# Spreading 1/std of the large layer norms: two rounded products of 512 columns and diagonal parts from VectorE, in place of four full products of 128

## The chip, the cores and the metric

One core of one Trainium2 chip. The metric is the time of one execution in device microseconds (us). Names of engines: PE is TensorE (PEld its weight loads), DVE is VectorE, ACT is ScalarE, POOL is GpSimd, SP is SyncE.

## The reference

Input x is 32 batches x 32 tokens x 256 channels, cond is 32 x 256. In short:

```python
x = x + conv(x, cond)                       # each batch causal, 32 lags, one weight per channel and lag
ada = cond @ ada_w + ada_b                  # shift1, scale1, gate1, shift2, scale2, gate2
x1 = ln(x) * (1 + scale1) + shift1          # ln(x) = (x - mean) * rsqrt(var + 1e-6) over 256 channels
q, k, v = split(x1 @ qkv_w + qkv_b)         # 16 heads of 128
x = x + gate1 * (attention(q, k, v) @ out_w + out_b)
x2 = ln(x) * (1 + scale2) + shift2
x = x + gate2 * (gelu(x2 @ ffn_w1 + b1) @ ffn_w2 + b2)
# and the block's result is added to its input once more
```

## The kernel before

Activations lie transposed: 128 channels on the partitions, tokens in the columns, two channel tiles (`ct` 0 and 1). The 1024 tokens are worked on in two halves of 512. A layer norm therefore sums over partitions, and does it with matrix products.

Large products are done in three rounded products each (`three`, L943 to L947; `v_tile` L949 to L956): weights and activations are split into a high part rounded to fp32r and a low part (`wh`, `wl`, `x1h`, `x1l`, `oh`, `ol`, `hh`, `hl`), and high x low, low x high and high x high are added in PSUM. ACT makes the high parts, POOL the low parts of the weights (L294) and of half of the hidden tiles (L332), DVE the low parts of the activations.

There are five norms. Norms 0 and 1 take 256 tokens each and the change leaves them alone. Norms 2, 3 and 4 take 512 tokens each ("large"): norm 2 is the first norm of the second half of the tokens, norms 3 and 4 are the second norm of the first and the second half. A large norm goes through these steps:

- `mean(n)` (L886): four rounded products of `ones_r` (every element 1/256) with high and low input parts, L894, put the mean into all partitions of a PSUM bank. `centre(n)` (L574, DVE) subtracts it, `squares(n)` (ACT, L388) squares.
- `var(n)` (L904): small products on PE, then on DVE `var_eps(n)` (L588): a transpose (L594) into `vt` and an addition (L597), so that `ve` holds var + eps of 512 tokens as 128 partitions x 4.
- `rstd(n)` (L301, POOL): power of -0.5 by L304, into `rs`, 128 x 4.
- `spread(n)` (L918, PE): for each of 4 columns k one full fp32 product of 128 columns, L925, with `rs[:, k]` broadcast as weights and the unit matrix `ident` moving. It puts 1/std of 512 tokens into all partitions of the bank.
- DVE: `norm(n)` multiplies (L604), `shift(n)` adds (L611), and after ACT's `x1_high(n)` (L398) `x1_low(n)` subtracts (L623). `scale_up(n)` (L585) has been done earlier.

Every engine has its own program, written out by hand in its order, and they meet at counting semaphores. PE's order around a spread: norms 2 and 3 are worked in between products of other work in rounds U = 3 and U = 5 of the loop at L1077 (`attend`, `var`, `out_proj(U-1, 0)`, `attend(U-1, 3)`, `out_proj(U-1, 1)`, `spread`, `out_proj(U-1, 2)`). Norm 4 lies in the second product of the feed-forward part for the first half (L1172 to L1180):

```python
for k in range(MT):            # MT = 8
    ffn2(0, k)
    ffn2(1, k)                 # 6 products of 512 columns for each k
    if k == 1: var(4)
    if k == 3: spread(4)
ffn1(1, range(MT))             # waits for x1_low(4), both channel tiles
```

On DVE the order is `var_eps`, `o_low` twice (L671), `norm` for norms 2 and 3, and `hidden_low(0, 7)`, `var_eps(4)`, `norm(4)` for norm 4. On POOL `rstd(2)` and `rstd(3)` stand ahead of the low parts of the next round's query weights, `rstd(4)` ahead of `hidden_low(1, 0)`. SP only starts loads and stores.

Of the kernel before, what the change touches and what calls it, by code (L numbers as in the profile page):

```python
# [5 lines left out]
F32 = mybir.dt.float32  # L6
F32R = mybir.dt.float32r
ALU = mybir.AluOpType
# [3 lines left out]
P = 128  # L12
# [4 lines left out]
def cond_resid_block_kernel(nc, x, cond, ada_w, ada_b, qkv_w, qkv_b, out_w, out_b,  # L17
# [5 lines left out]
    B, T, C = x.shape  # L23
# [8 lines left out]
    TG = HT // P  # L32
# [24 lines left out]
    NORMS = CHUNKS + [(0, HT), (HT, HT)]  # L57
# [13 lines left out]
    with ExitStack() as ctx:  # L71
        def sb(name, shape, dt=F32):
            return ctx.enter_context(nc.sbuf_tensor(name, shape, dt))

        def sem(name):
            return ctx.enter_context(nc.semaphore(name))
# [3 lines left out]
        x1h = sb("x1h", [P, CT, TOK], F32R)  # L80
        x1l = sb("x1l", [P, CT, TOK], F32R)
# [11 lines left out]
        ident = sb("ident", [P, P])  # L93
        ones = sb("ones", [P, P])
        ones_r = sb("ones_r", [P, P], F32R)
# [8 lines left out]
        rc = sb("rc", [P, GH * TG])  # L104
        ve = sb("ve", [P, TG])
        rs = sb("rs", [P, TG])
        mhalf = sb("mhalf", [P, TG])
        vt = sb("vt", [P, TG, T])

# [32 lines left out]
        s_in, s_mean, s_xm, s_sq = sem("ln_input"), sem("ln_mean"), sem("ln_centred"), sem("ln_squares")  # L142
        s_var, s_ve, s_rs, s_rb = sem("ln_var"), sem("ln_var_eps"), sem("ln_rstd"), sem("ln_rstd_spread")
        s_vt = sem("ln_var_transposed")
        s_sc, s_mod, s_x1f = sem("ln_scaled"), sem("ln_normed"), sem("x1_full")
        s_hi, s_lo = sem("x1_high"), sem("x1_low")
        s_whi = [sem(f"{n}_weights_high") for n in ("q", "k", "v", "o")]
# [13 lines left out]
        def part(t, ct, span):  # L161
            return t[:, ct, span[0]:span[0] + span[1]]
# [14 lines left out]
        def ln_c(n, ct):  # L177
            return part(yacc if n < NC else x0, ct, NORMS[n])
# [6 lines left out]
        STAT_BANK = [S_BANK, S_BANK, S_BANK, S_BANK, OB[0]]  # L185
# [89 lines left out]
        @block.gpsimd  # L275
        def _(g):
            g.memset(ident[:, :], 0.0).then_inc(s_id0, 1)
            g.wait_ge(s_id0, 1)
            g.affine_select(out=ident[:, :], in_=ident[:, :], compare_op=ALU.not_equal, fill=1.0,
                            base=0, pattern=[[-1, P]], channel_multiplier=1).then_inc(s_const, 1)  # L280
            g.memset(ones[:, :], 1.0 / C).then_inc(s_const, 1)
            g.memset(mhalf[:, :], -0.5).then_inc(s_const, 1)
            g.wait_ge(s_const, 3)

            g.wait_ge(s_cond, 1)
            for d, ct in BY_POOL:
                j = DIAG_LAGS[d]
                g.tensor_scalar(diag[:, CT * d + ct, :], ident[:, :], condT[:, ct, T - 1 - j:T - j], 0.0,
                                ALU.mult, ALU.add).then_inc(s_diag[1], 1)

            def low_part(U, p):
                i, cols = p // 2, slice(PIECE * p, PIECE * (p + 1))
                g.wait_ge(s_whi[i], 2 * U + p % 2 + 1)
                g.tensor_tensor(wl[:, cols], raw[:, cols], wh[:, cols].bitcast(F32), ALU.subtract)\  # L294
                    .then_inc(s_wlo[i], 1)

            def low_parts(U, i):
                low_part(U, 2 * i)
                low_part(U, 2 * i + 1)

            def rstd(n):  # L301
                nt = NORMS[n][1] // P
                g.wait_ge(s_ve, n + 1)
                g.tensor_tensor(rs[:, 0:nt], ve[:, 0:nt], mhalf[:, 0:nt], ALU.pow).then_inc(s_rs, 1)  # L304


            g.wait_ge(s_in, CT)
            low_parts(0, 0)
            low_part(0, 2)
            rstd(0)  # L310
            low_part(0, 3)
            g.wait_ge(s_lo, CT)
            low_part(0, 4)
            rstd(1)
            low_part(0, 5)
            low_parts(0, 3)
            g.memset(pt[:, :, :, :], 0.0).then_inc(s_zero, 1)
            for i in range(3):
                low_parts(1, i)
            for U in range(1, NU):  # L320
                if U == 3:
                    rstd(2)
                if U == 5:
                    rstd(3)
                low_parts(U + 1, 0)
                low_parts(U + 1, 1)
                low_parts(U, 3)
                low_parts(U + 1, 2)

            def hidden_low(n, m):  # L330
                g.wait_ge(s_hhi, MT * n + m + 1)
                g.tensor_tensor(hl[:, m, :], hf[:, m % 4, :], hh[:, m, :].bitcast(F32), ALU.subtract)\  # L332
                    .then_inc(s_hlo[0], 1)

            for m in (0, 2):
                hidden_low(0, m)
            low_parts(NU, 3)
            for m in (4, 6):
                hidden_low(0, m)
            rstd(4)  # L340
            for m in (0, 2, 4, 6):
                hidden_low(1, m)
# [187 lines left out]
        def _(v):  # L530
# [57 lines left out]
            def var_eps(n):  # L588
                v.wait_ge(s_var, n + 1)
                if n < 2:  # L590
                    nt = NORMS[n][1] // P
                    v.tensor_scalar(ve[:, 0:nt], STAT_BANK[n][:, 0:nt], EPS, None, ALU.add).then_inc(s_ve, 1)
                else:
                    v.transpose(vt[:, :, :], STAT_BANK[n][:, 0:P].rearrange("p (k r) -> p k r", r=T))\  # L594
                        .then_inc(s_vt, 1)
                    v.wait_ge(s_vt, n - 1)
                    v.tensor_scalar(ve[:, :], vt[:, :, 0:1].rearrange("p k r -> p (k r)"), EPS, None, ALU.add)\  # L597
                        .then_inc(s_ve, 1)

            def norm(n):  # L600
                v.wait_ge(s_rb, n + 1)
                v.wait_ge(s_sc, CT * (n + 1))
                for ct in range(CT):
                    v.tensor_tensor(ln_c(n, ct), ln_c(n, ct), STAT_BANK[n][:, 0:NORMS[n][1]], ALU.mult)\  # L604
                        .then_inc(s_mod, 1)

            def shift(n):
                for ct in range(CT):
                    v.wait_ge(s_mod, CT * n + ct + 1)
                    c = by_batch(ln_c(n, ct))  # L610
                    v.tensor_tensor(c, c, ada(SHIFT1 if n < NC else SHIFT2, ct, NORMS[n]), ALU.add)\  # L611
                        .then_inc(s_x1f, 1)
# [55 lines left out]
            def o_low(U, h):  # L668
                v.wait_ge(s_ohi, GH * U + h + 1)
                row = B_V + GH * (U % NG) + h  # L670
                v.scalar_tensor_tensor(out=ol[:, h, :], in0=OB[h % 2][:, :], scalar=bT[:, row:row + 1],  # L671
                                       in1=oh[:, h, :].bitcast(F32), op0=ALU.add, op1=ALU.subtract)\
                    .then_inc(s_olo, 1)
# [84 lines left out]
            scale_up(2)  # L758
            var_eps(2)
            o_low(2, 2)  # L760
            o_low(2, 3)
            norm(2)
            shift(2)
            x1_low(2)
# [15 lines left out]
            scale_up(3)  # L780
            var_eps(3)
            o_low(4, 2)
            o_low(4, 3)
            norm(3)
            shift(3)
# [19 lines left out]
            def hidden_low(n, m):  # L805
                v.wait_ge(s_hhi, MT * n + m + 1)
                v.tensor_tensor(hl[:, m, :], hf[:, m % 4, :], hh[:, m, :].bitcast(F32), ALU.subtract)\
                    .then_inc(s_hlo[1], 1)
# [11 lines left out]
            scale_up(4)  # L820
            hidden_low(0, 7)
            var_eps(4)
            norm(4)
            shift(4)
            x1_low(4)
# [30 lines left out]
        def _(pe):  # L856
            pe.wait_ge(s_const, 1)
            pe.wait_ge(s_row[0], 16)
            for ct in range(CT):
                m = pe.transpose(S_BANK[:, B * ct:B * (ct + 1)], crow[:, ct * P:(ct + 1) * P], ident[0:B, 0:B])  # L860
            m.then_inc(s_condt, 1)
            for n in range(2):
                t0, nt = CHUNKS[n][0] // P, CHUNKS[n][1] // P
                pe.wait_ge(s_x[n], 16)
                for ct in range(CT):
                    for t in range(nt):
                        m = pe.transpose((OB, YB)[n][ct][:, t * P:(t + 1) * P], xtok[:, t0 + t, ct * P:(ct + 1) * P], ident[:, :])  # L867
# [48 lines left out]
                m.then_inc(s_var, 1)  # L916

            def spread(n):  # L918
                pe.wait_ge(s_rs, n + 1)
                for k in range(NORMS[n][1] // P):  # L920
                    if n < 2:
                        dst = STAT_BANK[n][:, k * P:(k + 1) * P]
                    else:
                        dst = STAT_BANK[n][:, :].rearrange("p (t k r) -> p k t r", t=TG, r=T)[:, k]
                    m = pe.matmul(dst, rs[:, k:k + 1].to_broadcast([P, P]), ident[:, :], start=True, stop=True)  # L925
                m.then_inc(s_rb, 1)

# [114 lines left out]
            for ct in range(CT):  # L1042
                for t in range(TG):
                    m = pe.transpose(OB[ct][:, t * P:(t + 1) * P], xtok[:, TG + t, ct * P:(ct + 1) * P], ident[:, :])
# [127 lines left out]
            for k in range(MT):  # L1172
                if k == MT // 2:
                    pe.wait_ge(s_wlo[3], 2 * NU + 2)
                ffn2(0, k)
                ffn2(1, k)
                if k == 1:
                    var(4)
                if k == 3:
                    spread(4)  # L1180
            ffn1(1, range(MT))
            pe.wait_ge(s_fin, CT)
# [49 lines left out]
```

## Time and profile before

| what | value |
|---|---|
| median of 3 runs | 312.3 us (312.1 to 313.58) |
| the profiled execution | 311.81 us |
| its span, first to last instruction | 310.0 us |
| PE busy | 298.0 us (96%) |
| PEld busy | 251.9 us |
| DVE busy | 180.2 us |
| ACT busy | 174.5 us |
| POOL busy | 120.4 us |
| granted TensorE clock | 1.000 |

Busy times overlap; an engine's time counts only where the others wait for it. The duration of a matrix product in a row is longer than the distance from its start to the next start, because products are pipelined: distances of starts are what PE's time is made of. A full fp32 product shows as two rows each of PE and PEld.

### The profile page before, as it was taken

To read this page: it belongs to the slowest core of one execution; us is meant where nothing else is said; L and a number is where in the kernel's file an instruction comes from. 1 tells how busy PE (TensorE), PEld (TensorE's weight loads), DVE (VectorE), ACT (ScalarE), POOL (GpSimd) and SP (SyncE) were. 2 spreads that over 40 slices of the span, in tenths; PEclk is the share of its full clock that TensorE was granted. 3 is DMA by queue.
4 is the path that set the end of the run, shared out by engine and by line. 5 is a ranking of instruction groups with operands and counts; after the bars stand their busy time and mean duration, and the time that the engine had idled before them with its cause. 6 is when DMAs were issued, how large, how long until landed. Compare 5 with 4: busy or idle time off the path is not lost.

```text
span 310.0 us, 6149 instructions
## 1 busy us (share of the span) xinstructions
PE 298.0 (96%) x2604; PEld 251.9 (81%) x2604; DVE 180.2 (58%) x303; ACT 174.5 (56%) x316; POOL 120.4 (39%) x103
## 2 busy tenths in 40 slices
PE   4978999999999999999999999999999999899995
PEld 3875997878898888788888888888898888678885
DVE  3997698987866745472546554341620556957232
ACT  5752568434762855486376736644762794625901
POOL 5007729331911544072337305531821671611400
PEclk9999999999999999999999999999999999999999
DMA  7903321400160061007004300610150020000012
GB/s 231 362 27 79 112 84 57 150 0 2 43 231 0 2 229 45 0 4 271 1 2 153 120 2 2 213 59 2 59 212 2 2 68 3 0 0 3 0 68 68
DMA packets 15259, 23.00 MB, mean 74 GB/s; under 512 B 792, under 2 KB 8320, under 8 KB 15232
## 3 DMA queue, kind: packets, MB, share of 16 engines
q1 hardware_dynamic: 15184, 22.58, 21.6%
q8 instruction: 20, 0.33, 0.4%
q10 hardware_dynamic: 48, 0.03, 0.1%
q14 instruction: 7, 0.06, 0.1%
HBM read 21.57 MB, written 1.05 MB: 73 GB/s over the span
## 4 chain that ended last, share of the span: by engine, by line
PE 85%; DVE 9%; POOL 3%; ACT 1%; DMA 1%; issue 1%; DVEq 0%; POOLq 0%
PE bank L945 18%; PE bank L947 18%; PE bank L946 18%; PE bank L1019 9%; DVE xc L548 6%; PE bank L953 5%; PE bank L954 4%; PE bank L955 4%; PE bank L1003 3%; POOL wl L294 3%; PE bank L925 1%; DVE x1l L617 1%; PE bank L894 1%; DMA crow<-in_cond_dram 1%; PE bank L867 1%
## 5 line engine op out<-in xcount | busy, mean ns | idle before, releaser
L294 POOL TENSOR_TENSOR wl<-raw,wh 128x512 fp32r<-128x512 f32 x72 | 98.7, 1398 | 133.2 <-ACT wh L357 116.5
L408 ACT ACTIVATE pool<-bank,bT 128x512 f32<-128x512 f32 x56 | 38.5, 688 | 54.3 <-PE bank L947 54.3
L945 PE MATMUL bank<-x1h,wl 128*128 128x512 f32 (+1 forms) x176 | 66.3, 377 | 0.8 <-DVE x1l L623 0.4
L947 PE MATMUL bank<-x1h,wh 128*128 128x512 f32 (+1 forms) x176 | 65.1, 370 | 0.0
L946 PE MATMUL bank<-x1l,wh 128*128 128x512 f32 (+1 forms) x176 | 65.1, 370 | 0.0
L671 DVE SCALAR_TENSOR_TENSOR ol<-bank,bT,oh 128x512 fp32r<-128x512 f32 x32 | 24.0, 750 | 36.6 <-ACT oh L433 35.6
L357 ACT ACTIVATE wh<-raw 128x512 fp32r<-128x512 f32 x72 | 40.9, 621 | 3.5 <-PE bank L947 3.5
L548 DVE SCALAR_TENSOR_TENSOR xc<-x,condT,xc 128x496 f32<-128x496 f32 (+27 forms) x82 | 42.8, 592 | 0.1
L945 PEld LDWEIGHTS bank<-x1h,wl 128*128 128x128 f32 x176 | 33.2, 188 | 7.1 <-DVE x1l L623 0.8
L947 PEld LDWEIGHTS bank<-x1h,wh 128*128 128x128 f32 x176 | 33.2, 188 | 5.7
L946 PEld LDWEIGHTS bank<-x1l,wh 128*128 128x128 f32 x176 | 33.2, 189 | 5.4
L1019 PEld LDWEIGHTS bank<-pt,pool 128*128 128x128 f32 x256 | 32.1, 191 | 2.0 <-issue 0.3
L1019 PE MATMUL bank<-pt,pool 128*128 128x128 f32 x256 | 32.5, 275 | 0.0
L433 ACT ACTIVATE oh<-bank,bT 128x512 fp32r<-128x512 f32 x32 | 22.0, 686 | 10.0 <-PE bank L1019 10.0
L945 PE MATMUL bank<-oh,wl 128*128 128x512 f32 x64 | 26.8, 418 | 0.2 <-DVE ol L671 0.2
L953 PE MATMUL bank<-wh,x1l 128*128 128x512 f32 x64 | 25.9, 404 | 0.0
L947 PE MATMUL bank<-oh,wh 128*128 128x512 f32 x64 | 25.1, 392 | 0.0
L946 PE MATMUL bank<-ol,wh 128*128 128x512 f32 x64 | 25.0, 390 | 0.0
L954 PE MATMUL bank<-wl,x1h 128*128 128x512 f32 x64 | 24.9, 389 | 0.0
L955 PE MATMUL bank<-wh,x1h 128*128 128x512 f32 x64 | 24.9, 389 | 0.0
L643 DVE TENSOR_REDUCE mx<-bank 128x16 f32<-128x512 f32 x8 | 5.5, 692 | 32.4 <-PE bank L1003 32.4
L666 DVE STREAM_TRANSPOSE pt<-pnorm 32x512 f32<-32x512 f32 (+1 forms) x36 | 23.2, 644 | 1.2
(121 smaller groups left out, 421.5 us busy)
## 6 DMA issues: line engine op xcount, KB each, us to landing
raw<-in_L_cond_qkv_w_dram SPq DMA_DIRECT2D x24, 512.0 KB, 5.6
raw<-in_L_cond_out_w_dram SPq DMA_DIRECT2D x8, 512.0 KB, 3.7
raw<-in_L_cond_ffn_w_dram SPq DMA_DIRECT2D x4, 512.0 KB, 5.1
adaw<-in_L_cond_ada_w_dram SPq DMA_DIRECT2D x1, 1024.0 KB, 10.8
out_dram<-pool SPq DMA_DIRECT2D x3, 256.0 KB, 2.2
pool<-in_x_dram SPq DMA_DIRECT2D x2, 256.0 KB, 3.1
adaw<-in_L_cond_ada_w_dram SPq DMA_DIRECT2D x1, 512.0 KB, 5.4
pool<-in_x_dram SPq DMA_DIRECT2D x1, 512.0 KB, 6.2
```

Of the source, the lines that this page charges most:

```text
L294: g.tensor_tensor(wl[:, cols], raw[:, cols], wh[:, cols].bitcast(F32), ALU.subtract)\
L357: a.activation(wh[:, cols], raw[:, cols], ACT.Copy).then_inc(s_whi[i], 1)
L408: a.activation((q_sb if j < GH else k_sb)[:, j % GH, :], src, ACT.Identity, bias=bias(U, j // GH, j % GH)).then_inc(s_ev, 1)
L548: m = v.scalar_tensor_tensor(out=acc[:, :, j:], in0=xs[:, :, :T - j], scalar=w, in1=(acc if i else xs)[:, :, j:], op0=ALU.mult, op1=ALU.add)
L671: v.scalar_tensor_tensor(out=ol[:, h, :], in0=OB[h % 2][:, :], scalar=bT[:, row:row + 1], in1=oh[:, h, :].bitcast(F32), op0=ALU.add, op1=A ...
L945: pe.matmul(dst, wl[:, w_cols], a_hi, start=start, stop=False)
L946: pe.matmul(dst, wh[:, w_cols], a_lo, start=False, stop=False)
L947: return pe.matmul(dst, wh[:, w_cols], a_hi, start=False, stop=stop)
L953: pe.matmul(dst, x1l[:, kt, tk], wh[:, wc], start=(kt == 0), stop=False)
L954: pe.matmul(dst, x1h[:, kt, tk], wl[:, wc], start=False, stop=False)
L955: m = pe.matmul(dst, x1h[:, kt, tk], wh[:, wc], start=False, stop=(kt == CT - 1))
L1019: m = pe.matmul(OB[h % 2][:, t * P:(t + 1) * P], v_sb[:, t, h * P:(h + 1) * P], pt[:, h, t, :], start=True, stop=True)
```

## The change

For norms 2 to 4 `spread(n)` becomes two rounded products of 512 columns: `ones_r` as weights and, moving, a matrix that carries 1/std times 256 on a diagonal for each of the 4 columns, once its high part (in `x1h`) and once its low part (in `x1l`), added in PSUM. DVE makes these in a new `rstd_diagonal(n)`: `rsh` = 256 rs rounded, `rsl` the rest, and `ident` times each of them, spread over 512 columns. For norms 2 and 3 `rstd_diagonal` stands between the two last `o_low`, for norm 4 behind `var_eps(4)`. POOL waits behind `rstd(n)` until both diagonal parts are written. In the feed-forward part `spread(4)` moves from behind k == 3 to behind k == 4. Norms 0 and 1 are as before.

```diff
@@ gpsimd
                 g.tensor_tensor(rs[:, 0:nt], ve[:, 0:nt], mhalf[:, 0:nt], ALU.pow).then_inc(s_rs, 1)
+                if n >= 2:
+                    g.wait_ge(s_rd, 2 * (n - 1))
@@ vector
+            def rstd_diagonal(n):
+                v.wait_ge(s_rs, n + 1)
+                v.tensor_scalar(rsh[:, :], rs[:, :], float(C), None, ALU.mult).then_inc(s_rh, 1)
+                v.wait_ge(s_rh, n - 1)
+                v.scalar_tensor_tensor(out=rsl[:, :], in0=rs[:, :], scalar=float(C), in1=rsh[:, :].bitcast(F32),
+                                       op0=ALU.mult, op1=ALU.subtract).then_inc(s_rl, 1)
+                eye = ident[:, :].rearrange("p (t r) -> p t r", r=T).unsqueeze(2).to_broadcast([P, TG, TG, T])
+                for t, r in ((x1h, rsh), (x1l, rsl)):
+                    if r is rsl:
+                        v.wait_ge(s_rl, n - 1)
+                    dst = part(t, 0, NORMS[n]).rearrange("p (t k r) -> p t k r", t=TG, r=T)
+                    by_k = r[:, :].bitcast(F32).unsqueeze(1).unsqueeze(3).to_broadcast([P, TG, TG, T])
+                    v.tensor_tensor(dst, eye, by_k, ALU.mult).then_inc(s_rd, 1)
...
             o_low(2, 2)
+            rstd_diagonal(2)
             o_low(2, 3)
...
             o_low(4, 2)
+            rstd_diagonal(3)
             o_low(4, 3)
...
             var_eps(4)
+            rstd_diagonal(4)
             norm(4)
@@ tensor
             def spread(n):
+                if n >= 2:
+                    for i, t in enumerate((x1h, x1l)):
+                        pe.wait_ge(s_rd, 2 * (n - 2) + i + 1)
+                        m = pe.matmul(STAT_BANK[n][:, :], ones_r[:, :], part(t, 0, NORMS[n]),
+                                      start=(i == 0), stop=(i == 1))
+                    m.then_inc(s_rb, 1)
+                    return
                 pe.wait_ge(s_rs, n + 1)
...
-                if k == 3:
+                if k == 4:
                     spread(4)
```

The order of the instructions at norm 2 on DVE (`ol` is the low part of the attention output, `yacc` the working copy in the norm), first before, then with the change:

```order
L597 TENSOR_SCALAR ve<-vt 128x4 [waits ln_var_transposed]
L671 SCALAR_TENSOR_TENSOR ol<-bank,bT,oh 128x512 [waits attn_out_high] x2
L604 TENSOR_TENSOR yacc<-yacc,bank 128x512 [waits ln_scaled,ln_rstd_spread]
L604 TENSOR_TENSOR yacc<-yacc,bank 128x512
L611 TENSOR_TENSOR yacc<-yacc,adaT 128x512 [waits ln_normed] x2
```

```order
L603 TENSOR_SCALAR ve<-vt 128x4 [waits ln_var_transposed]
L693 SCALAR_TENSOR_TENSOR ol<-bank,bT,oh 128x512 [waits attn_out_high]
L610 TENSOR_SCALAR rsh<-rs 128x4 [waits ln_rstd]
L612 SCALAR_TENSOR_TENSOR rsl<-rs,rsh 128x4 [waits ln_rstd_high]
L620 TENSOR_TENSOR x1h<-ident,rsh 128x512
L620 TENSOR_TENSOR x1l<-ident,rsl 128x512 [waits ln_rstd_low]
L693 SCALAR_TENSOR_TENSOR ol<-bank,bT,oh 128x512 [waits attn_out_high]
L626 TENSOR_TENSOR yacc<-yacc,bank 128x512 [waits ln_scaled,ln_rstd_spread]
L626 TENSOR_TENSOR yacc<-yacc,bank 128x512
```

Four DVE instructions came in ahead of the last `ol`.

The order on PE at norm 4 (`hh`, `hl` are the hidden activations), before and with the change:

```order
L945 MATMUL bank<-hh,wl 128x512 [waits hidden_low_odd]
L946 MATMUL bank<-hl,wh 128x512
L947 MATMUL bank<-hh,wh 128x512
L925 MATMUL bank<-ident,rs 128x4x32 [waits ln_rstd]
L925 MATMUL bank<-ident,rs 128x4x32 x3
L945 MATMUL bank<-hh,wl 128x512 [waits hidden_low_even,o_weights_low]
```

```order
L974 MATMUL bank<-hh,wl 128x512 [waits hidden_low_even,o_weights_low]
L975 MATMUL bank<-hl,wh 128x512
L976 MATMUL bank<-hh,wh 128x512
L974 MATMUL bank<-hh,wl 128x512 [waits hidden_low_even]
L975 MATMUL bank<-hl,wh 128x512
L976 MATMUL bank<-hh,wh 128x512
L947 MATMUL bank<-x1h,ones_r 128x512 [waits ln_rstd_on_diagonal]
L947 MATMUL bank<-x1l,ones_r 128x512 [waits ln_rstd_on_diagonal]
```

The spread moved behind six products of `ffn2` that stood behind it.

On POOL the instruction behind the power of norm 2, the same at norm 3, with the change:

```order
L307 TENSOR_TENSOR rs<-ve,mhalf 128x4 [waits ln_var_eps]
L297 TENSOR_TENSOR wl<-raw,wh 128x512 [waits q_weights_high,ln_rstd_on_diagonal]
L297 TENSOR_TENSOR wl<-raw,wh 128x512 [waits q_weights_high]
```

The first low part of the weights now waits for the diagonal parts too.

## Rows read from the trace of the kernel before

**Rows 1.** The page: busy time of PE, and the chain by engine.

```profile
PE 298.0 (96%) x2604; PEld 251.9 (81%) x2604; DVE 180.2 (58%) x303; ACT 174.5 (56%) x316; POOL 120.4 (39%) x103
...
PE 85%; DVE 9%; POOL 3%; ACT 1%; DMA 1%; issue 1%; DVEq 0%; POOLq 0%
```

**Rows 2.** Busy time by stretch: us, then each engine's busy us, clock, DMA.

```profile
112.00:130.00 18.00, 18.00 (x113) 15.40 (x112) 9.67 (x16) 9.07 (x15) 3.58 (x4) 1.00 0.28 99
170.00:190.00 20.00, 20.00 (x244) 16.96 (x243) 9.46 (x17) 11.00 (x18) 4.50 (x4) 1.00 0.15 56
```

**Rows 3.** Timeline of PE at norm 2's spread: start, us, instruction.

```profile
122.03 0.40 PE L947 MATMUL bank<-oh,wh 128*128 128x512 f32 x1
122.27 1.05 PE L925 MATMUL bank<-ident,rs 128*128 128x128 f32 x8
...
123.39 0.39 PE L946 MATMUL bank<-ol,wh 128*128 128x512 f32 x1
```

**Rows 4.** Timeline of PE at norm 2's mean.

```profile
111.74 0.39 PE L894 MATMUL bank<-x1h,ones_r 128*128 128x512 f32 x1
111.96 0.61 PE L894 MATMUL bank<-x1l,ones_r 128*128 128x512 f32 x2
112.42 0.39 PE L945 MATMUL bank<-x1h,wl 128*128 128x512 f32 x1
```

**Rows 5.** Timeline of DVE and POOL at norm 2.

```profile
118.63 0.32 DVE L594 STREAM_TRANSPOSE vt<-bank 128x128 f32<-128x128 f32 x1 [0.20 <-PE bank L914]
118.98 0.17 DVE L597 TENSOR_SCALAR ve<-vt 128x4 f32<-128x4 f32 x1
119.06 0.75 DVE L671 SCALAR_TENSOR_TENSOR ol<-bank,bT,oh 128x512 fp32r<-128x512 f32 x1
121.80 0.75 DVE L671 SCALAR_TENSOR_TENSOR ol<-bank,bT,oh 128x512 fp32r<-128x512 f32 x1 [1.99 <-ACT oh L433]
...
119.23 1.01 POOL L304 TENSOR_TENSOR rs<-ve,mhalf 128x4 f32<-128x4 f32 x1 [7.16 <-DVE ve L597]
120.21 2.53 POOL L294 TENSOR_TENSOR wl<-raw,wh 128x512 fp32r<-128x512 f32 x2
132.76 2.55 POOL L294 TENSOR_TENSOR wl<-raw,wh 128x512 fp32r<-128x512 f32 x2 [10.02 <-ACT wh L357]
```

**Rows 6.** Timeline of PE, POOL and DVE at norm 3.

```profile
178.52 1.05 PE L925 MATMUL bank<-ident,rs 128*128 128x128 f32 x8
...
175.49 1.01 POOL L304 TENSOR_TENSOR rs<-ve,mhalf 128x4 f32<-128x4 f32 x1 [7.16 <-DVE ve L597]
```

**Rows 7.** Timeline of PE at norm 4, and the first product that needs its result.

```profile
275.44 1.05 PE L925 MATMUL bank<-ident,rs 128*128 128x128 f32 x8
...
276.56 0.40 PE L946 MATMUL bank<-hl,wh 128*128 128x512 f32 x1
...
281.84 0.40 PE L945 MATMUL bank<-x1h,wl 128*128 128x512 f32 x1
```

**Rows 8.** Timeline of DVE and POOL at norm 4.

```profile
276.53 1.29 DVE L604 TENSOR_TENSOR x<-x,bank 128x512 f32<-128x512 f32 x2 [2.57 <-PE bank L925]
...
279.12 1.30 DVE L623 TENSOR_TENSOR x1l<-x,x1h 128x512 fp32r<-128x512 f32 x2
...
274.04 1.01 POOL L304 TENSOR_TENSOR rs<-ve,mhalf 128x4 f32<-128x4 f32 x1 [4.88 <-DVE ve L597]
```

**Rows 9.** Timeline where PE did wait for a low part: DVE, then PE.

```profile
30.43 0.76 DVE L623 TENSOR_TENSOR x1l<-yacc,x1h 128x256 fp32r<-128x256 f32 x2
...
31.25 0.38 PE L945 MATMUL bank<-x1h,wl 128*128 128x256 f32 x1 [0.45 <-DVE x1l L623]
31.47 0.28 PE L946 MATMUL bank<-x1l,wh 128*128 128x256 f32 x1
```

**Rows 10.** Timeline of DVE and POOL ahead of norm 4's mean.

```profile
264.83 3.18 DVE L617 TENSOR_TENSOR x1l<-yacc,x1h 128x512 fp32r<-128x512 f32 x2 [0.21 <-ACT x1h L393]
262.33 3.44 POOL L294 TENSOR_TENSOR wl<-raw,wh 128x512 fp32r<-128x512 f32 x2 [6.67 <-ACT wh L357]
```

More of the change, by code:

```diff
@@ L106, in cond_resid_block_kernel @@
         rs = sb("rs", [P, TG])
+        rsh = sb("rsh", [P, TG], F32R)
+        rsl = sb("rsl", [P, TG], F32R)
         mhalf = sb("mhalf", [P, TG])
@@ L144, in cond_resid_block_kernel @@
         s_vt = sem("ln_var_transposed")
+        s_rh, s_rl, s_rd = sem("ln_rstd_high"), sem("ln_rstd_low"), sem("ln_rstd_on_diagonal")
         s_sc, s_mod, s_x1f = sem("ln_scaled"), sem("ln_normed"), sem("x1_full")
@@ L918, in spread @@
             def spread(n):
+                if n >= 2:
[5 more added lines that the diff above has]
+                    return
                 pe.wait_ge(s_rs, n + 1)
                 for k in range(NORMS[n][1] // P):
[L921 to L924, printed above, removed]
+                    dst = STAT_BANK[n][:, k * P:(k + 1) * P]
                     m = pe.matmul(dst, rs[:, k:k + 1].to_broadcast([P, P]), ident[:, :], start=True, stop=True)
```

## The prediction

> **What bounds the kernel now.** I read the page first: PE is busy for 298.0 of 310.0 us, and 85% of the chain that ended last is PE's [rows 1]. What matters is whether it is so at the three places of the change, so the table of stretches comes next: around norms 2 and 3 PE is busy for 18.00 of 18.00 and 20.00 of 20.00 us, at the full clock [rows 2]. In these stretches a microsecond taken from PE's queue is a microsecond of the kernel, unless PE then waits for somebody. Last I read the timelines at each norm, PE first, then DVE and POOL, and looked for the slack that the new instructions may use up.
>
> **What PE loses.** Norm 2 shows the price of the old spread by starts: from the start of the last product ahead of it (122.03) to the start of the second product behind it (123.39) pass 1.36 us, and in it lie that product, the spread, and one product behind it [rows 3]. A rounded product of 512 columns takes one start to the next in 0.23 us: the last three of the mean's four take 0.68 with the first, (112.42 - 111.74) / 3 = 0.227, three starts being visible [rows 4]; those with `ones_r` as weights are exactly the new kind. Four intervals (the product ahead, two of the new spread, one behind) are 0.92, so a spread saves 1.36 - 0.92 = 0.44 us. The old spread at norm 3 has the same 1.05 row [rows 6], and norm 4 shows 275.44 to 276.56, 1.12 for spread and one product, against 3 x 0.23 = 0.69: 0.43 [rows 7]. **Three spreads: minus 1.31 us**, all of it on PE's queue.
>
> **What DVE gains, norms 2 and 3.** POOL's power ends at 119.23 + 1.01 = 120.24 [rows 5]. From DVE to POOL a result takes 0.08 (118.98 + 0.17 = 119.15 to 119.23); I take the same back: DVE starts at 120.32. `rsh` is an instruction on 128 x 4 like `ve`, 0.17, to 120.49; a dependent one starts 0.03 later (118.95 to 118.98), an independent one 0.08 behind the start before it (118.98 to 119.06) [rows 5]. So `rsl` starts at 120.52 and the first product with `ident` at 120.60. These two have no row. The nearest is a DVE product or subtraction on 128 x 512, 0.69 for one and 1.29 for two in a row, so 0.60 from start to start [rows 8]. The far end is such an instruction next to a busy POOL, 3.18 for two, 1.59 each [rows 10]. I take 0.69 and 0.60, since POOL is made to wait and is idle then. The parts are written at 121.29 and 121.89. PE wants them at 122.27 and 122.50, and loads the weights of a product about one interval, 0.23, ahead; even the second weight load, at 122.27, is 0.33 after PE can know (121.89 + 0.05, the way of 31.19 to 31.25 in [rows 9]). The last `o_low` can start at 121.80, just behind, as before [rows 5]: it waited there for ACT for 1.99 us, and this wait is the cover of all four new instructions. Gone, each norm would cost about what DVE runs over. Norm 3 has the same distances, its power at 175.49 and its spread at 178.52 (3.03, against 3.04 at norm 2) [rows 6]. **Zero at both.**
>
> **What POOL's wait costs.** Behind it stand two low parts of query weights, now at 120.21 [rows 5]; they go back to 121.95, 1.7 us later, and end near 124.5. The next POOL work comes at 132.76, after 10.02 us of idle time [rows 5], and these weights are for the next round. DVE's shift instructions at norm 2 will start near 124.2 and may meet the last of it; by the rate of [rows 10] that is 0.9 us at most on a result which the next round needs. SP's next load of these weights stands behind another wait in the same queue. **Zero.**
>
> **Norm 4** has least room. POOL's power ends at 275.05 [rows 8]; by the same steps the parts are written at 276.10 and 276.70. PE's place for the spread is now six products later: 275.44 + 6 x 0.23 = 276.81. The first product is in time; the second's weight load is due at 276.81, and PE can know at 276.75. It fits with 0.06 to spare. Without the move to k == 4 PE would have waited 1.3 us here. The second product starts at 277.04, its row lasts 0.39 [rows 4], so DVE's norm starts at about 277.47 in place of 276.53 [rows 8]: 0.94 later. The last low part then ends at 279.12 + 1.30 + 0.94 = 281.36 in place of 280.42. The product that waits for it was due at 281.84 [rows 7], and now is at 281.84 - 0.44 = 281.40, with its weight load at 281.17. PE knows at 281.42. A product that had to wait this way started its stream late: at norm 0 the next start came 0.22 behind, where 0.12 is usual [rows 9], so 0.10. It starts at 281.52 instead of 281.40: **plus 0.12 us**. So the move takes 1.42 us of slack almost exactly. DVE's next steps (sums and gating for the first half) are 0.9 later too, but PE needs them only behind eight more tiles.
>
> **The sum:** -1.31 + 0.12 = -1.2 us. Against the profiled execution, 311.81, that is 310.6; its own time lies 0.5 below the median of the runs, 312.3, and against that median it is **311.1 us**, 0.4% less.
>
> **A rule weighed against a row.** Two DVE instructions in a row overlap by 0.09 us (1.29 for two of 0.69) [rows 8]. The Trainium skill, VectorE: DVE Perf Modes, section "The DRAIN you can't avoid", says that the next operation does not start before the pipe has emptied (and that an operation not held may start earlier). By that the second diagonal part of norm 4 would be there 0.09 later, PE would wait by about 0.13 for it, and the sum would be -1.1; by the row it is -1.2. I keep the row.
>
> **Rivals.**
>
> A. *The diagonal parts are late and PE waits at all three spreads* (slower). Each part reads `ident` in a pattern that repeats and one value per 32 columns, a form without a row here; if it costs d, then at norms 2 and 3 the second is written 2d after 120.60, PE waits from d = 0.84 on, and at norm 4 from 0.67 on. Six parts: the waits come to 6d - 4.7, and pass the 1.2 saved at about d = 1.0. At the far end of 1.59 [rows 10] they are 4.8, less 1.2, so about 315.9. For it: nothing but the missing row; against it: DVE's instructions of 512 columns all take about 0.69 while POOL rests, and broadcast operands (`adaT`, L611) stand among them. From 1.0 us on it decides; chance 0.07.
>
> B. *The gain is half eaten at norm 4*: PE waits 0.3 to 1.0 us for the second part or for the last low part, because slack there is 0.06 at one place and -0.25 at the other. Any 0.1 to 0.3 us that I missed on the chain POOL, DVE, PE, DVE, ACT, DVE counts in full: 311.4 to 312.1. For it: the rows leave no room; against: only one place of three. Chance 0.16.
>
> C. *A collision falls otherwise*: ahead of norm 4's mean DVE takes 3.18 us for two subtractions beside a POOL that works from 262.33 to 265.77, and PE stands [rows 10]. They start within fractions of a microsecond of each other, and one of the two at 0.69 would bring PE forward by 0.9: -2.1, so 310.2. The Trainium skill, SBUF — State Buffer, section "Who interferes with whom", has it that the order of issue decides which of the two engines blocks; this row shows a block of 0.9 for each, and none that fell the other way. For it: the phase may change; against: everything there is started by PE, so the shift of 0.88 keeps the distances. Chance 0.10.
>
> **How the numbers follow.** The forecast (310.8 to 311.4) has 0.67; a median may lie 0.3 off on top of that. The unknown costs: if the far end of a part (1.59) holds, that is rival A; the near end is in the sum, and nothing excludes 0.1 of extra gain. A measurement of this kernel can tell about 0.5%, 1.6 us, from no change. Faster by that: rival C, and a few of the forecast's cases with luck in the median, 0.13. Slower: A, 0.06 with a rest. All else is within 0.5%, 0.81. The range of 8 in 10 takes in C and most of B and the scatter of medians of some 0.3: 310.1 to 312.3.
>
> **What would show it.** The two new product rows 0.23 apart, no PE wait for a diagonal part, at norm 2 the last `o_low` still at its distance of 3.1 us from the transpose of the variance; two DVE rows of 0.69 for `x1h` and `x1l` from `ident`; PE's weight load for the first feed-forward product of the second half waiting for DVE's low part by 0.1 to 0.3 us; span 308.8. Wrong would be: DVE rows above 0.85 (A), a PE wait above 0.5 at norm 4 (B), a different length of the two DVE subtractions ahead of norm 4's mean (C).

## The result, and the profile of the changed kernel

| | before | changed |
|---|---|---|
| median | 312.31 us (16 runs, 311.72 to 313.58) | **314.36 us** (16 runs, 311.72 to 316.59) |
| ratio | 1 | **1.0049** [1.0031, 1.0067] |
| profiled execution, its span, granted clock | 311.81, 310.0, 1.000 | 315.42, 313.6, 0.989 |

Slower by 0.5%, where 311.1 us (310.1 to 312.3) was forecast. The page of the changed kernel, its busy times, the queue that brings in instructions and the chain by engine (to be held against [rows 1]):

```profile
PE 300.4 (96%) x2586; PEld 253.4 (81%) x2586; DVE 185.7 (59%) x315; ACT 174.6 (56%) x316; POOL 121.0 (39%) x103
...
q8 instruction: 20, 0.33, 0.5%
...
PE 85%; DVE 8%; POOL 3%; issue 1%; ACT 1%; DMA 1%; DVEq 0%; POOLq 0%
```

PE issues 18 products and 18 weight loads fewer and is nevertheless busy for 2.4 us more. The three places of the change do not explain that. Norm 3 (to be held against [rows 6]), PE, then DVE, then POOL (start, duration, instruction, idle time before it and its releaser):

```profile
178.66 0.40 PE L976 MATMUL bank<-oh,wh 128*128 128x512 f32 x1
178.90 0.39 PE L947 MATMUL bank<-x1h,ones_r 128*128 128x512 f32 x1
179.13 0.39 PE L947 MATMUL bank<-x1l,ones_r 128*128 128x512 f32 x1
179.35 0.39 PE L974 MATMUL bank<-oh,wl 128*128 128x512 f32 x1
...
176.90 0.17 DVE L610 TENSOR_SCALAR rsh<-rs 128x4 fp32r<-128x4 f32 x1 [0.47 <-POOL rs L307]
177.11 0.16 DVE L612 SCALAR_TENSOR_TENSOR rsl<-rs,rsh 128x4 fp32r<-128x4 f32 x1
177.19 0.68 DVE L620 TENSOR_TENSOR x1h<-ident,rsh 128x512 fp32r<-128x512 f32 x1
177.79 0.68 DVE L620 TENSOR_TENSOR x1l<-ident,rsl 128x512 fp32r<-128x512 f32 x1
...
178.55 2.55 POOL L297 TENSOR_TENSOR wl<-raw,wh 128x512 fp32r<-128x512 f32 x2 [1.68 <-DVE x1l L620]
```

The two products start 0.23 apart and wait for nobody, the diagonal parts take 0.68 each, 0.60 from start to start, and POOL stands back for 1.68 us: all as forecast. Norm 4 (against [rows 7, 8]), DVE and PE, and the first product that needs its result:

```profile
279.69 0.69 DVE L620 TENSOR_TENSOR x1l<-ident,rsl 128x512 fp32r<-128x512 f32 x1
...
280.62 0.40 PE L947 MATMUL bank<-x1h,ones_r 128*128 128x512 f32 x1
280.85 0.39 PE L947 MATMUL bank<-x1l,ones_r 128*128 128x512 f32 x1
...
285.05 0.40 PE L976 MATMUL bank<-hh,wh 128*128 128x512 f32 x1
285.28 0.43 PE L974 MATMUL bank<-x1h,wl 128*128 128x512 f32 x1
285.56 0.39 PE L975 MATMUL bank<-x1l,wh 128*128 128x512 f32 x1
```

No wait at the spread; at the first feed-forward product of the second half the next start comes 0.28 later in place of 0.23, so 0.05 is lost.

To find the 3.6 us by which the span is longer I laid the two PE timelines side by side and took the start of the same product in both:

| place | before | changed | difference |
|---|---|---|---|
| a product at 34 us, long before the change's first place | 33.59 | 34.46 | +0.87 |
| second product behind the spread of norm 2 | 123.39 | 123.81 | +0.42 |
| second product behind the spread of norm 3 | 179.64 | 179.58 | -0.06 |
| last product ahead of the scores of round U = 5 | 187.39 | 187.29 | -0.10 |
| first product behind these scores | 188.93 | 190.97 | **+2.04** |
| 13 products later | 192.00 | 195.63 | **+3.63** |
| ahead of norm 4's spread | 274.52 | 278.30 | +3.78 |
| behind it | 277.72 | 281.08 | +3.36 |
| last tiles | 297.79 | 301.30 | +3.51 |

The spreads bring -0.45, -0.48 and -0.42, together -1.35 (the second product behind is taken, because before the first one after a full spread still takes 0.31 to the next start in place of 0.23). The loss arises in the attention scores of round 5, 128 small products in 1.2 us that the change does not touch, and right behind them. PE there, before and changed:

```profile
187.71 1.30 PE L1003 MATMUL bank<-pool 128*32 128x32 f32 x128
188.93 0.51 PE L953 MATMUL bank<-wh,x1l 128*128 128x512 f32 x1
```

```profile
187.60 1.26 PE L1032 MATMUL bank<-pool 128*32 128x32 f32 x125
190.78 0.25 PE L1032 MATMUL bank<-pool 128*32 128x32 f32 x3 [1.92 <-issue]
190.97 0.50 PE L982 MATMUL bank<-wh,x1l 128*128 128x512 f32 x1
...
192.23 0.62 PE L984 MATMUL bank<-wh,x1h 128*128 128x512 f32 x1
192.64 0.63 PE L982 MATMUL bank<-wh,x1l 128*128 128x512 f32 x1
```

After 125 of the 128 products PE stands for 1.92 us, and the releaser is "issue": no engine and no transfer of data that the profile knows of. A little later products of 0.39 take 0.63 and start 0.43 apart in place of 0.23. The table of stretches of the changed kernel (us, PE busy, PEld, DVE, ACT, POOL, granted clock, DMA share, GB/s) shows both causes:

```profile
188.00:188.50 0.50, 0.50 (x80) 0.50 (x72) 0.00 (x0) 0.50 (x2) 0.00 (x0) 1.00 0.16 33
188.50:189.00 0.50, 0.37 (x45) 0.26 (x31) 0.00 (x0) 0.50 (x2) 0.09 (x1) 1.00 0.00 0
189.00:189.50 0.50, 0.00 (x0) 0.00 (x0) 0.00 (x0) 0.34 (x1) 0.50 (x1) 1.00 0.00 0
...
192.00:192.50 0.50, 0.50 (x3) 0.46 (x2) 0.49 (x1) 0.00 (x0) 0.00 (x0) 0.73 0.00 0
192.50:193.00 0.50, 0.50 (x2) 0.38 (x2) 0.00 (x0) 0.48 (x1) 0.00 (x0) 0.50 0.00 0
195.50:196.00 0.50, 0.50 (x3) 0.36 (x3) 0.47 (x2) 0.50 (x1) 0.50 (x2) 0.86 0.00 0
```


First, just behind the start of the scores a transfer begins; then PE stands, from 188.86 to 190.78. Second, from about 192.2 to 195.6, behind this standstill, the granted clock is 0.50, the lower of the two levels (1.2 of 2.4 GHz), which costs the 1.6 us between +2.04 and +3.63. The remaining +0.87 at 34 us is an early delay with a clock of 0.84 from 25 to 30 us; the same kernel's second profile below is without it (33.59, as before), and b_diag below, whose PE does the work of before, is 2.47 behind at 33 us with a clock of 1.00, so I count early delays as scatter.

Which transfer? The view of the DMA queues from 187 to 191 us shows one packet of the queue of instructions (16 KB; 20 such packets carry PE's program: 0.33 MB) in the slice from 188.1 on (each GB/s number is a fortieth of the stretch; the last row is the queue's packets, MB and share), and none from 178 to 187 us:

```profile
GB/s 0 0 0 0 0 0 0 0 0 0 0 164 0 0 0 0 0 0 0 0 0 0 0 0 0 0 0 0 0 0 0 0 0 0 0 0 0 0 0 0
...
q8 instruction: 1, 0.02, 2.1%
```

Before, the view from 178 to 183 us has the corresponding packet at 179.9, 7.8 us ahead of the same scores, and none from 186 to 190:

```profile
GB/s 0 0 0 0 0 0 0 0 0 0 0 0 0 0 0 131 0 0 0 0 0 0 0 0 0 0 0 0 0 0 0 0 0 0 0 0 0 0 0 0
...
q8 instruction: 1, 0.02, 1.1%
```

This gave **theory S** (stream): PE's program comes in blocks of 16 KB. Each product is two instructions (a PE and a PEld row), a full fp32 product four; each large spread so went from 16 instructions to 4. Norms 2 and 3 put the code of the scores of round 5 24 instructions earlier in the stream. These scores run 256 instructions in 1.2 us, and now the fetch of the block in which they end starts only with them (0.6 us behind their first product, where it was 7.8 us ahead of it before). The Trainium skill, Runtime: NRT & Kernel Launch, section "Instruction fetch mechanics", describes such blocks of 256 instructions and calls the cost of crossing a boundary "mostly hidden"; here it is not.

### The profile page after: what moved, and what is told of

Its sections match the earlier page's. It is cut to its first block, busy times and chain, and to the rows that moved or that the text cites. A ratio compares the mean times of both kernels' runs of the same rounds, so it can differ in the third digit from the quotient of the medians.

```text
span 313.6 us, 6128 instructions
## 1 busy us (share of the span) xinstructions
PE 300.4 (96%) x2586; PEld 253.4 (81%) x2586; DVE 185.7 (59%) x315; ACT 174.6 (56%) x316; POOL 121.0 (39%) x103
## 4 chain that ended last, share of the span: by engine, by line
PE 85%; DVE 8%; POOL 3%; issue 1%; ACT 1%; DMA 1%; DVEq 0%; POOLq 0%
PE bank L974 18%; PE bank L976 18%; PE bank L975 18%; PE bank L1048 9%; DVE xc L554 6%; PE bank L982 5%; PE bank L984 5%; PE bank L983 4%; PE bank L1032 3%; POOL wl L297 3%; DVE x1l L639 1%; PE bank L919 1%; DMA crow<-in_cond_dram 1%; PE bank L892 1%; PE bank L939 1%
## 5 line engine op out<-in xcount | busy, mean ns | idle before, releaser
L984 PE MATMUL bank<-wh,x1h 128*128 128x512 f32 x64 | 25.6, 400 | 0.0
```

What stands on the lines that cost most here:

```text
L984: m = pe.matmul(dst, x1h[:, kt, tk], wh[:, wc], start=False, stop=(kt == CT - 1))
```

## The experiments

All were timed against before on the chip they ran on. Twelve kernels in three jobs; before had 311.86 us in the first job, 312.66 in the second, 312.86 in the third (29, 35 and 35 runs), its fastest 311.68, 311.94 and 311.92. Many executions, of before too, carry early delays of 1 to 2.5 us, ahead of every place of the change, so beside medians I give the fastest runs where they lie close together. `s_fill` is a semaphore that nobody waits for; adding to it does no work and takes one place in PE's instruction stream.

**1. a_same**, the changed kernel again.

> The changed kernel once more, as the control. Theory S (the code stream of PE): the 24 machine instructions that PE no longer has before the attention scores of round U = 5 move these scores against the 16 KB blocks in which PE's code is fetched, so that one fetch starts only inside the scores and PE stands about 1.9 us there, and TensorE's clock falls to half for 3.4 us behind it. It then expects the stall at the scores of U = 5 in this profile too, and a time 1 to 3 us above before. Rival R (chance of a run: DMA, start of the early norms): no stall at that place in this profile, or one at another place, and the same in before's.

Measured: 313.83 us median, ratio 1.0051 [1.0024, 1.0079], so the loss repeats on another chip. PE's timeline:

```profile
186.88 1.26 PE L1032 MATMUL bank<-pool 128*32 128x32 f32 x125
189.69 0.25 PE L1032 MATMUL bank<-pool 128*32 128x32 f32 x3 [1.54 <-issue]
```

PE stands behind the same 125th product. The same products against before: -0.83 at the last product ahead of the scores, +0.94 at the first behind them, so the standstill costs 1.77. The clock stays at 1.00 here; it fell in the profile where the wait was 1.92.

**2. a_fill12**: in `three`, one addition in front of each of the 12 products behind each spread of norms 2 to 4, so that PE's stream is as long as before's ahead of the scores.

```diff
@@ spread(n), n >= 2
+                    fillers[0] += 12
+            def filler():
+                if fillers[0]:
+                    fillers[0] -= 1
+                    pe.sem_inc(s_fill, 1)
@@ three
+                filler()
```

> The changed kernel with 12 additions to an unused semaphore on PE's queue, one by one between the 12 products behind each of the three spreads, so that every later instruction of PE stands at the same number in its queue as before the change. Theory S: no stall at the scores of U = 5, no fall of the clock there, and the saving of PE appears, 311.0 to 311.6 us with before at 312.3, so 0.7 to 1.3 us below before and 2 to 4 below the changed kernel. Rival R, or a theory in which the work of VectorE or the new products slow the kernel: the time stays that of the changed kernel, 313 to 315.

Measured: 314.45 us, ratio 1.0062 [1.0036, 1.0087]. This expectation failed: PE still stands.

```profile
189.15 1.16 PE L1044 MATMUL bank<-pool 128*32 128x32 f32 x113
191.96 0.23 PE L1044 MATMUL bank<-pool 128*32 128x32 f32 x4 [1.65 <-issue]
```

But the place is telling. 24 instructions are more in front of it (two spreads), and PE stands behind the 113th product in place of the 125th: 12 products, 24 instructions, earlier. So the standstill belongs to a fixed place in the instruction stream. The fetch still started with the scores (its packet at 189.5). So the place of the boundary alone does not say when the fetch starts.

**3. b_start232**: the kernel before with 232 additions at the head of PE's queue.

```diff
@@ tensor
+            for _ in range(232):
+                pe.sem_inc(s_fill, 1)
```

> The kernel before, its work untouched, with 232 additions to an unused semaphore at the very start of PE's queue, where PE waits 3.4 us for its first input; with blocks of 256 instructions this puts the scores of U = 5 at the same place in a block as in the changed kernel (24 less), without the change. Theory S: a stall of about 1.9 us at the scores of U = 5 and the clock at half behind it, 314 to 316 us. If the additions take longer than the cover, up to 2 us more at the start, seen there. Theories that lay it to the new work: no stall at these scores.

Measured: 348.63 us (346.89 to 350.64); the additions took far more than I had allowed for, PE's first product starts at 36.65 in place of 3.40 us. The time is useless, the timeline is not. Around round 5 no instruction of the change is in the kernel, and PE does this:

```profile
220.93 1.26 PE L1006 MATMUL bank<-pool 128*32 128x32 f32 x125
223.84 0.25 PE L1006 MATMUL bank<-pool 128*32 128x32 f32 x3 [1.64 <-issue]
```

Against the changed kernel 232 + 24 = 256 instructions more lie ahead of this place: exactly one block. **The standstill was put into before's work by the position of its code**; the additions also start all work 33 us later, but that alone would not choose the same 125th product. Theory S holds for the cause.

**4. a_start24**: the changed kernel with 24 additions at the head of PE's queue, where PE waits for the first load anyway.

> The changed kernel with 24 additions to an unused semaphore at the start of PE's queue: scores of U = 5 stand in their block as before the change, the scores of the earlier rounds 12 or 24 instructions later than before. Theory S: no stall at U = 5 and 310.9 to 311.6 us, unless the shift makes a stall in another round, which the profile would show in its scores. Others: 313 to 315.

Measured: 312.25 us, ratio 1.0008 [0.9986, 1.0031]. The scores run through (188.86, x128), with the fetch at 181.5. The first product starts at 4.62 in place of 3.40, so the additions outran their cover by 1.22 us and ate the gain.

**5. b_diag**: before's PE, with DVE's `rstd_diagonal` and POOL's wait, whose results nobody reads (spread behind k == 3).

> VectorE's and GpSimd's part of the change alone: rstd_diagonal and GpSimd's wait are in, the results of it are not read; PE's queue is that of the kernel before (four full products, behind k == 3). Theory S (PE's code stream and its block boundary in the scores of U = 5): as before, within 0.3 us (the norm of n = 4 starts some 0.2 us later on VectorE, within its slack), no stall in the scores of U = 5. Rival V (VectorE's work, or the stopped GpSimd, costs the time): 313 to 314.5.

Measured: 314.16 us (312.26 up; one run at 373.78), ratio 1.0018 [0.9992, 1.0044]: not to be told from before. Its fastest three, 312.26 to 312.38, are 0.3 above before's fastest; the interval alone would still admit 1.4 us. The profile narrows it: its PE is 2.47 us behind before's at 33 us, ahead of every place of the change, 2.42 behind at the scores of round 7, and 2.68 at the last product. So the DVE and POOL parts cost PE nothing up to norm 4 and at most some 0.25 there, and no standstill occurs.

**6. a_pe**: only PE's part. The two products are released by `rs` and multiply what lies in `x1h` and `x1l`, so 1/std is not spread in this kernel.

> PE's part of the change alone: two rounded products behind k == 4 whose moving data is whatever x1h and x1l hold, released by rs as before the change; no rstd_diagonal, no wait on GpSimd, so 1/std of the norms 2 to 4 is not spread and the output is not the reference's. Theory S: PE's queue counts the same instructions as in the changed kernel, so the stall at the scores of U = 5 is there and the time is that of the changed kernel, 312.4 to 314.5. Rival V: without VectorE's work the saving of 1.2 us appears, 310.7.

Measured: 313.2 us, ratio 0.9998 [0.9972, 1.0024], 11 of 12 runs from 312.74 up and one at 310.92. PE stands after 125 of the 128 products, for 1.82 us from start to start. DVE, POOL and their waits are not needed for the standstill. By the ratio this kernel is neither slower nor faster than before, so the saving of 1.2 us that rival V wanted is not there either; in the profile, which has next to no early delay, its last product comes 1.11 us behind before's, as in a_same (0.97).

**7. a_start8** and **8. a_start14**: as 4, with 8 and 14 additions.

> The changed kernel with 8 additions to an unused semaphore at the start of PE's queue, under the cover of PE's wait for its first input (24 of them outran it by 1.2 us, so up to about 15 are free). The block boundary, at which PE stood behind 250 instructions of the scores of U = 5, comes 8 instructions earlier against the program, behind 242. Theory S: if the boundary ahead of the scores now lies in front of a wait that PE's queue passes early, no stall and 310.6; if not, the stall as in the changed kernel but in front of 14 instead of 6 instructions, 312.4 to 314.5. It shows how far the boundary must move.

> The same with 14 additions, still nearly under the cover: boundary behind 236 instructions of the scores of U = 5. Theory S: no stall, since 24 showed none, and without what 24 cost at the start: 310.5 to 310.8 us, 1.2 less than before; the scores of U = 6 and 7 stay free of a stall too. Rival V: 313 to 314.

Measured: 8: 313.95 us, ratio 1.0016 [0.9985, 1.0048]; one run of 12 at 310.91, the others from 312.82 up, though the profile, at 313.44 us, was without a standstill: it is 2.44 us behind before at 33 us already and only 1.61 behind at the last product. So a run above 312.8 need not be one with a standstill. 14: **311.89 us, ratio 0.9970 [0.9944, 0.9995]**; the first product starts at 3.37, so the additions are hidden, and four runs lie at 310.92 to 311.01.

**9. a14_again**, the same as 8 in its own job.

> The version with 14 semaphore additions at the start of PE's queue once more, with more rounds. Theory S (the changed kernel's whole loss is PE's standstill inside the scores of round 5, which depends on where that code lies in PE's instruction stream): median 0.8 to 1.3 us under before, ratio 0.996 to 0.9975, and no product of the scores waiting over 1 us with nobody named. Rival (the earlier 0.997 was scatter between runs): ratio 0.999 to 1.001.

Measured: **311.79 us, ratio 0.9969 [0.9946, 0.9992]**, five of 12 runs at 310.93 to 311.02 where before's fastest are 311.92 to 312.06. The scores run through:

```profile
188.90 1.30 PE L1035 MATMUL bank<-pool 128*32 128x32 f32 x128
```

So the version with 14 additions beats both kernels, by 0.3% of before and, by the ratios to before, 0.8% of the changed kernel.

**10. a8_again**, 8 additions once more, to see whether one kernel can go both ways.

> The version with 8 additions at the start once more. If the code boundary near the scores of round 5 is marginal there, its single runs fall in two groups, one near 310.9 (no standstill) and one from 312.4 up (standstill of 1.7 to 1.9 us): ratio 1.000 to 1.004. Rival (8 additions are as good as 14 and the earlier runs were scatter): ratio 0.996 to 0.998.

Measured: 314.54 us, ratio 1.0053 [1.0033, 1.0072], none of 12 runs below 313.82. The expectation of two groups failed within this job: all 12 are late. That one kernel can go both ways is shown by the two profiles, 7 without and this one with a standstill:

```profile
186.85 1.23 PE L1035 MATMUL bank<-pool 128*32 128x32 f32 x121
190.01 0.27 PE L1035 MATMUL bank<-pool 128*32 128x32 f32 x7 [1.94 <-issue]
```

8 instructions more in front, 4 products fewer ahead of the standstill: 121 = 125 - 4, the rule of experiment 2 once more. Here again the wait was over 1.9 us, and again the clock fell behind it:

```profile
191.50:192.00 0.50, 0.50 (x2) 0.40 (x2) 0.25 (x1) 0.21 (x1) 0.00 (x0) 0.50 0.00 0
```

**11. a14_k3**: 14 additions, the spread of norm 4 back behind k == 3.

> As a14_again, but the spread of norm 4 back behind k == 3. By the prediction's steps PE then waits at norm 4 until the second diagonal part is written, 1.2 to 1.4 us, and gets back what it no longer waits for the last low part (0.12) with the norm started earlier: span 1.1 to 1.3 us above a14_again, ratio to before 1.000 to 1.001. Rival (PE has other slack there, so the move is worth nothing): within 0.3 us of a14_again.

Measured: 312.32 us, ratio 0.9979 [0.9957, 1.0002]; the fastest 311.88, so 0.95 above the fastest of a14_again (the medians differ by 0.5). PE waits for both diagonal parts:

```profile
274.44 0.40 PE L979 MATMUL bank<-hh,wh 128*128 128x512 f32 x1
275.27 0.49 PE L950 MATMUL bank<-x1h,ones_r 128*128 128x512 f32 x1 [0.43 <-DVE x1h L621]
275.87 0.50 PE L950 MATMUL bank<-x1l,ones_r 128*128 128x512 f32 x1
276.20 0.39 PE L977 MATMUL bank<-hh,wl 128*128 128x512 f32 x1
```

1.76 us from the last product ahead to the first behind, in place of 3 x 0.23: 1.07 lost. The move to k == 4 is worth about 1 us and is what lets norm 4 gain at all; the ratio lies lower than expected (0.9979 where 1.000 to 1.001 was put), the distance of the fastest runs near what was expected (1.1 to 1.3).

**12. a14_free**: 14 additions, without POOL's wait behind the power.

```diff
@@ gpsimd
-                if n >= 2:
-                    g.wait_ge(s_rd, 2 * (n - 1))
```

> As a14_again, but without POOL's wait behind the power. If POOL and DVE hinder each other as ahead of norm 4's mean in before (1.59 per DVE subtraction beside a busy POOL), the two diagonal parts take 1.2 to 1.6 us each in place of 0.68 at norms 2 and 3, the second is there 1.1 to 1.8 us later, and PE waits 0.5 to 1.4 us at each of the two: ratio 1.000 to 1.005. Rival (only luck of phase makes them collide): rows of 0.68 and the time of a14_again.

Measured: 314.63 us, ratio 1.0062 [1.0042, 1.0083]; fastest 314.24, 3.3 above the fastest of a14_again. The wait is worth 3 us, but the rows are not those that I expected. Norm 2, DVE, POOL, PE:

```profile
120.79 1.24 DVE L608 TENSOR_SCALAR rsh<-rs 128x4 fp32r<-128x4 f32 x1 [0.47 <-POOL rs L308]
122.06 1.20 DVE L610 SCALAR_TENSOR_TENSOR rsl<-rs,rsh 128x4 fp32r<-128x4 f32 x1
123.19 0.68 DVE L618 TENSOR_TENSOR x1h<-ident,rsh 128x512 fp32r<-128x512 f32 x1
...
120.73 2.52 POOL L298 TENSOR_TENSOR wl<-raw,wh 128x512 fp32r<-128x512 f32 x2
...
122.55 0.40 PE L976 MATMUL bank<-oh,wh 128*128 128x512 f32 x1
123.92 0.50 PE L947 MATMUL bank<-x1h,ones_r 128*128 128x512 f32 x1 [0.97 <-DVE x1h L618]
124.53 0.50 PE L947 MATMUL bank<-x1l,ones_r 128*128 128x512 f32 x1
```

The two 128 x 512 parts take 0.68; it is the two instructions on 128 x 4 that go from 0.17 to 1.24 and 1.20, each the length of one POOL subtraction (2.52 / 2). The parts begin when POOL's two subtractions are just over (123.25), so this run does not show what they would take beside a busy POOL. PE loses (1.37 - 0.23) + (0.61 - 0.23) = 1.5 us at norm 2, and the same pair of gaps stands at norm 3. The Trainium skill, SBUF — State Buffer, section "Who interferes with whom", has it that a DVE instruction in a two-port mode (which a `tensor_scalar` can enter) and one with two SBUF inputs contend with GpSimd for a shared pair of ports, and that the side that issues first keeps it for its whole instruction. The trace agrees for both, `rsh` (`tensor_scalar`) and `rsl` (two inputs): each ends with the POOL subtraction beside it.

## Why the prediction was wrong

- **PE loses 1.31 us at three spreads**: right. -0.45, -0.48 and -0.42 in the changed kernel's profile, 1.35.
- **Zero at norms 2 and 3, fitting at norm 4, POOL's wait free**: right. No wait for a diagonal part; parts of 0.68 and 0.69, where 0.69 was taken; in b_diag these parts cost PE nothing up to norm 4, and the move to k == 4 is worth 1.07 at PE where 1.3 was put. At norm 4 the second part was written at 280.38 and its weight load was due at 280.62, 0.19 to spare where 0.06 was reckoned. Without POOL's wait the loss would have been 3 us: the prediction priced this wait at nothing, and did not say what it buys.
- **Plus 0.12 for the last low part of norm 4**: 0.05 at that product. The distance to before grows by another 0.1 up to the last tiles and 0.1 more to the last product; for that no row names a cause, but b_diag, with before's products, also falls back by 0.2 there, so it does not come from the new spread.
- **The sum, -1.2 us**: near what the edit is worth when the standstill is kept away. a_start14 and a14_again give -1.0 us between fastest runs and a ratio of 0.997, which is 1.0 us too; behind norm 4's spread the profiles lose 0.2 to 0.25 against before's, where the sum had 0.12.
- **The step that failed** is in the first part: "a microsecond taken from PE's queue is a microsecond of the kernel, unless PE then waits for somebody". PE waited for nobody; it waited for its own program. The sum counted what the edit takes from PE's queue in time and never in instructions: 36 fewer, 24 of them ahead of the scores of round 5. A term for the fetch of instructions was missing, and none of the rivals contained it. A falls with the parts of 0.68 (its condition at norms 2 and 3 should read 0.81, not 0.84: the 0.05 from DVE to PE was left out), B with the missing waits at norm 4, and the two DVE subtractions ahead of norm 4's mean again took 3.18, so C did not occur either. The time came out on A's side of before without any of A's mechanism.
- **The size**: in the profile 2.14 us for the standstill (-0.10 to +2.04) and 1.6 for the clock behind it, which the prediction took as full throughout; in a_same 1.77 and nothing. At the last product, without the early delay, this leaves +2.8 in the changed kernel's profile and +1.0 in a_same's, and the medians lay 1.5 (ratio) to 2.0 us above before.

**What stays open.** Where PE stands is settled; why the fetch starts early or late is not. The boundary ahead of the critical block lies 30 instructions before these scores in before (fetch 7.8 us early), and 6 in the changed kernel (fetch with the scores); ahead of the scores stands a product that waits. That PE's instruction reading runs ahead and stops at this wait, on the wrong side of the boundary, would fit 1, 3, 4, 6, 8 and 9 and the wavering of 8 additions (14 instructions), but a_fill12 has before's 30 and was late all the same. This explanation is only argued.

The scores of rounds 6 and 7 are the same code and bear on it: in the four profiles that had the boundary 6 instructions ahead of the scores in round 5 (changed, 1, 3 and 6) it lies 12 ahead in round 6, the packet starts 1.4 to 2.0 us ahead of the scores, and PE runs through; from 18 instructions on it starts 6.2 to 7.8 us ahead in every profile and round but a_fill12's round 5. So a few instructions decide, and the start of the fetch jumps by microseconds.

## What to carry to other kernels

Count an edit on a busy PE queue in instructions as well as in time: it shifts all the code behind it against the blocks in which the program is fetched, and a burst of very short products (here 256 instructions in 1.2 us) is the place where a late fetch shows, as a wait for "issue" with one packet of the instruction queue just ahead. If an edit that does all it should still loses, look for such a row first; a few additions to an unused semaphore, put where PE waits anyway, move the boundary and test it. And where POOL's work starts just as a short dependent chain on DVE does, try holding POOL back: here that was worth 3 us, and the chain's smallest instructions paid.

## What the runs showed of the hardware

- PE's standstill for its own program: 1.74 to 2.13 us from start to start in six profiles, at the 125th, 121st or 113th product of the scores, moving by one product for each two instructions put in front, and back again after 256. Its packet of 16 KB took 0.9 to 1.4 us and began 0.4 to 0.6 us behind the first product of the scores; PE went on 1.2 to 1.5 us after the packet's end.
- The granted clock fell to 0.50 for about 3.4 us behind the two waits of 1.92 and 1.94 us, and stayed at 1.00 behind those of 1.54 to 1.65 (four profiles).
- Additions to a semaphore in a row on PE's queue are not free: 232 of them moved the first product from 3.40 to 36.65 us, about 0.15 each; 14 fit into the first wait, 24 cost 1.22 us. Put one by one between products of 512 columns (a_fill12) they cost nothing that shows: the products behind norm 2's spread start 0.23 apart, as without them.
- DVE instructions on 128 x 4 took 1.24 and 1.20 us in place of 0.17 and 0.16 beside a POOL subtraction on 128 x 512 of 1.26.
